# Attention scores in 32x32 tiles, |Kh| steps on ScalarE, reordered engines and filler matmuls in a one-core transformer layer

## The reference

```python
g, v = x @ Wg.T + bg, x @ Wv.T + bv            # 16 heads of 8 features
corr = (g_i . g_j) / (|g_i| |g_j| + 1e-8) * m  # m: j <= i and j >= i - 128
corr = (corr + 1) / 2
gene_means = mean over j of corr;  denom = gene_means + 0.5
fitness = 1 / (denom * sum_i(1 / denom))
attn = softmax over j of (corr * fitness_i * m + (1 - m) * -1e10)
x1 = layernorm(x + (attn @ v) @ Wo.T + bo)
gate, up = fp4(x1) @ fp4(Wgate).T, fp4(x1) @ fp4(Wup).T   # 352 wide
h = silu(gate) * up
out = layernorm(x1 + fp4(h) @ fp4(Wdown).T)
```

## Time and profile before

| | |
|---|---|
| median of 3 runs | 390.52 us (386.58 to 390.61) |
| the profiled execution | 388.84 us, its span 387.0 us |
| PE busy | 329.3 us (85%), 2964 matmuls |
| DVE busy | 285.6 us (74%) |
| ACT busy | 223.8 us (58%) |
| POOL busy | 188.2 us (49%) |

### The profile page before, as it was taken

The page is one execution under the profiler, slowest core; times in us unless marked ns, Lnnn a source line. Parts: engine busy times, 40 slices in busy tenths (PEclk is TensorE's granted clock), DMA queues, the critical chain, the costliest instruction groups (busy, mean ns, idle before and its releaser), DMA issues.

```text
span 387.0 us, 8906 instructions
## 1 busy us (share of the span) xinstructions
PE 329.3 (85%) x2964; PEld 196.2 (51%) x2964; DVE 285.6 (74%) x820; ACT 223.8 (58%) x499; POOL 188.2 (49%) x466
## 2 busy tenths in 40 slices
PE   6368878798899999999999999999998999967542
PEld 4234444454455565655565555555554556635331
DVE  1535356667879797979797979797979798886751
ACT  2034564566667776767676767777776777513210
POOL 7754033507274747374737373737373333541441
PEclk9999998899999999999999999999999999985655
DMA  4001000000010101010101010100000000000000
GB/s 117 27 1 29 14 2 3 27 2 29 0 30 3 42 1 42 0 46 1 42 0 45 1 43 2 43 0 30 3 30 0 29 3 27 15 0 14 15 14 19
DMA packets 12405, 7.64 MB, mean 20 GB/s; under 512 B 1026, under 2 KB 12356, under 8 KB 12356
## 3 DMA queue, kind: packets, MB, share of 16 engines
q1 hardware_dynamic: 12356, 7.03, 6.4%
HBM read 4.93 MB, written 2.10 MB: 18 GB/s over the span
## 4 chain that ended last, share of the span: by engine, by line
PE 30%; DVE 23%; POOL 20%; issue 17%; ACT 8%; POOLq 0%; ACTq 0%; DVEq 0%
PE OT L745 6%; PE S L722 5%; PE WA L871 4%; POOL nt L463 4%; PE S L726 3%; ACT Pm L561 3%; POOL rstd L496 3%; POOL nt L465 3%; POOL rn L470 3%; POOL nt L468 2%; DVE A L1274 2%; POOL B L510 2%; DVE xn L1166 2%; PE WB L784 2%; DVE h L1118 2%
## 5 line engine op out<-in xcount | busy, mean ns | idle before, releaser
L561 ACT ACTIVATE Pm<-S 128x384 f32<-128x384 f32 x256 | 111.7, 490 | 64.0 <-PE S L726 63.9
L722 PE MATMUL S<-mask,ident 128*128 128x384 f16 x256 | 65.8, 340 | 10.0 <-ACT Pm L561 7.8
L745 PE MATMUL OT<-Pm,gv 128*32 128x256 f32 (+1 forms) x1024 | 56.8, 341 | 0.0
L487 POOL TENSOR_TENSOR hq<-hm,hs 128x352 f32<-128x352 f32 x32 | 25.2, 789 | 63.8 <-DVE hm L1136 63.6
L726 PE MATMUL S<-BT,AT 32*128 32x256 f16 (+1 forms) x512 | 44.3, 252 | 0.0
L745 PEld LDWEIGHTS OT<-Pm,gv 128*32 128x32 f32 x1024 | 27.2, 111 | 21.4 <-issue 6.0
L726 PEld LDWEIGHTS S<-BT,AT 32*128 32x128 f16 x512 | 14.4, 93 | 43.0 <-issue 43.0
L722 PEld LDWEIGHTS S<-mask,ident 128*128 128x128 f16 x256 | 18.9, 99 | 33.7 <-issue 14.8
L840 PE MATMUL WD<-wdT,hqT 128*128 128x128 f32 (+1 forms) x192 | 29.5, 311 | 1.5 <-ACT hqT L614 1.5
L840 PEld LDWEIGHTS WD<-wdT,hqT 128*128 128x128 f32 (+1 forms) x192 | 26.3, 217 | 4.1 <-ACT hqT L614 2.2
L1112 DVE SCALAR_TENSOR_TENSOR hh<-th,WC 128x352 f32<-128x352 f32 x29 | 15.0, 518 | 17.7 <-ACT th L585 17.6
(11 more groups left out here) (160 smaller groups left out, 724.4 us busy)
## 6 DMA issues: line engine op xcount, KB each, us to landing
xT<-x_turned_dram SPq DMA_DIRECT2D x16, 128.0 KB, 2.2
x_res<-x_dram SPq DMA_DIRECT2D x16, 128.0 KB, 2.1
out_dram<-yo SPq DMA_DIRECT2D x16, 128.0 KB, 2.1
wf<-w_down_dram SPq DMA_DIRECT2D x1, 176.0 KB, 2.6
wgv<-wgv_dram SPq DMA_DIRECT2D x1, 128.0 KB
wf<-w_gate_dram SPq DMA_DIRECT2D x1, 128.0 KB, 2.2
wf<-w_up_dram SPq DMA_DIRECT2D x1, 128.0 KB, 2.2
woT<-wo_dram SPq DMA_DIRECT2D x1, 64.0 KB
```

The lines of the kernel that those rows point to most:

```text
L487: pool.tensor_tensor(b3(hq[:, k, 0:I]), b3(hm[:, k]), bc(hs[:, k], QB), ALU.mult).then_inc(s_hq, 1)
L561: act.activation(Pm[:, group % PR, hd % 4, :], S[:, (H * x + hd) % 3, 0:SCW], ACT.Exp, scale=1.0 / ZS).then_inc(s_exp, 1)
L722: pe.matmul(S[:, bank, 0:SCW], ident16[:, :], mask16[:, :], start=True, stop=False)
L745: i = pe.matmul(OT[VP * g:VP * (g + 1), T - (q1 - q0):T], gv_flat[:, at:at + VP], Pm[:, (GROUPS * x + c) % PR, g, q0:q1], start=(kt == 0 a ...
```

## The change

Scores: instead of the mask over everything and two wide matmuls per head, each head takes twelve matmuls with 32 contraction rows and 32 output rows: for each 32 keys only the queries that the window lets them meet (160 columns for the first 128 keys, 128, 96, 64 and 32 for the second), and then a mask of three 32-column blocks for each 32 keys on top. What lies outside is never written: DVE sets it to -60000 once at the start. Rounding of h: ACT computes |2^22 * hn - 4| (hn has its sign turned over by a negative factor), and DVE needs two combined operations (max with the constant, then add or subtract) where it had four. Orders: POOL does all three Newton steps together, then the high half of B, then `rstd`, and both halves of `h_over_scale` later; ACT takes gsq and gv before values_out 0 and exponentials 6; DVE takes gh before the scale of h, the low half of A behind all of quant_x, and the three steps of gene_size in between those of the fitness, ahead of gate and up. `keep_busy` puts three 128x384 matmuls whose results are overwritten before the hq transposes, before the attention transpose, and before gate/up k=0.

```diff
+            def keep_busy(bank):
+                for _ in range(3):
+                    pe.matmul(bank[:, 0:SCW], ident16[:, :], mask16[:, :], start=True, stop=True)
...
             pair = [(2 * p + k, (H * x + 2 * p + k) % 3) for k in range(2)]
-            for hd, bank in pair:
-                pe.matmul(S[:, bank, 0:SCW], ident16[:, :], mask16[:, :], start=True, stop=False)
-            for kt, (q0, q1) in enumerate(((0, T), (T, SCW))):
+            for kt in range(NT):
                 for hd, bank in pair:
                     r, c = 32 * (hd % 4), hd // 4
-                    i = pe.matmul(S[:, bank, q0:q1], AT[r:r + 32, x % 2, c, kt * P:(kt + 1) * P],
-                                  BT[r:r + 32, x % 2, c, T - (q1 - q0):T], start=False, stop=(kt == 1))
-                    if kt == 1:
-                        i.then_inc(s_sc, 1)
+                    for k0 in range(0, P, KG):
+                        at, n = (k0, P + KG) if kt == 0 else (T + k0, P - k0)
+                        q = kt * P + k0
+                        pe.matmul(S[k0:k0 + KG, bank, at:at + n], AT[r:r + 32, x % 2, c, q:q + KG],
+                                  BT[r:r + 32, x % 2, c, q:q + n], start=(kt == 0), stop=False)
+            near = mask16[:, :].rearrange("p (b c) -> p b c", c=P)
+            for n, (hd, bank) in enumerate(pair):
+                m = 32 * (hd % 4)
+                for k0 in range(0, P, KG):
+                    i = pe.matmul(S[k0:k0 + KG, bank, 0:SCW].rearrange("p (b c) -> p b c", c=P)[:, :, k0:k0 + KG],
+                                  ident16[m:m + KG, m:m + KG], near[m:m + KG, :, m:m + KG],
+                                  start=False, stop=True)
+                i.then_inc(s_sc, 1)
...  PE's order
             scores(t, 2)
             after_last(pe, (t - 3, s_h, h_done(t - 3)))
+            keep_busy(WC)
             ... transposes of hq
             after_last(pe, *wc_last)
+            keep_busy(WC)
             pe.wait_ge(s_attn, t)
             ... transpose of attention
+            after_last(pe, (t - 4, s_ln2, 5 * (t - 4) + 1), (t - 3, s_h, h_done(t - 3)))
+            keep_busy(WD)
             pe.wait_ge(s_xac, copied(t) + (t == B))
-            after_last(pe, (t - 4, s_ln2, 5 * (t - 4) + 1), (t - 3, s_h, h_done(t - 3)))
...  POOL's order
-            newton(t + 2, (0, 1, 2) if t < 0 else (0,))
-            rstd(t - 2, ...)
+            newton(t + 2)
             B16 high half of t + 1
-            newton(t + 2, (1, 2))
-            h_over_scale(t - 3, 0)
+            rstd(t - 2, ...)
             A16 high half of t + 2
+            h_over_scale(t - 3, 0)
             h_over_scale(t - 3, 1)
             h_times_scale(t - 3, 0)
...  ACT
+            def step_of_h(x, k):
+                act.wait_ge(s_hn, NT * x + k + 1)
+                act.activation(hu[:, k], hn[:, k], ACT.Abs, bias=off[:, :], scale=STEP).then_inc(s_hu, 1)
             exps(t, 4)
+            step_of_h(t - 3, 0)
             BT copy of t + 1
+            step_of_h(t - 3, 1)
             exps(t, 5)
             xaT copy
-            values_out(t, 0)
-            exps(t, 6)
             gsq, gv of t + 3
+            values_out(t, 0)
+            exps(t, 6)
             tanh(t - 2, 0)
...  DVE: the old order and the new one, what moves
-  gate/up(t-3,1), h_scale 0, B low half, h_scale 1, gh, h_scale 2
+  gate/up(t-3,1), gh, h_scale 0, B low half, h_scale 1, h_scale 2
-  quant_x 0 to 5, A low half, quant_x 6 to 8, round_h(0) 4 steps
+  quant_x 0 to 8, A low half, round_h(0) 2 steps
-  gw, rs, den, rden; gate(t-2,0), gene_size 0, up(t-2,0), gene_size 1, 2
+  gene_size 0, gw, gene_size 1, rs, gene_size 2, den, rden; gate(t-2,0), up(t-2,0)
```

More of the change, by code:

```diff
@@ L32 @@
 MASKED = -60000.0
+KG = 32
 ZS = 256.0
@@ L35 @@
 UNNUDGE = 1.0 - 2.0 ** -22
+STEP, STEP_OFF = 2.0 ** 22, -4.0
 LN_EPS = 1e-5
@@ L236, in layer @@
         s_hrn = sem("s_hrn")
+        s_hu = sem("s_hu")
+        s_off = sem("s_off")
         s_hn = sem("s_hn")
@@ L450, in bias_rows, with newton @@
                 pool.wait_ge(c_pool, 30)
-            def newton(x, steps):
+            def newton(x):
                 y0 = rn[:, :]
@@ L456, in newton @@
                 sd = seed[:, :].bitcast(F32)
-                for k in steps:
+                for k in range(3):
                     src = sd if k == 0 else y0
@@ L510, in _ @@
                     pool.tensor_copy(B16[:, :, 0:3:2, :], twice(Bf)).then_inc(s_Bhi, 1)
-                if live(t + 2) and t >= 0:
-                    newton(t + 2, (1, 2))
-                if live(t - 3):
-                    h_over_scale(t - 3, 0)
+                if live(t - 2) and t != B + 1:
+                    rstd(t - 2, mv1, ve1, rstd1, nm1, nb1, s_ln1, 5 * (t - 2) + 5, s_rs1)
                 if live(t + 2):
@@ L574, in values_out @@
                 act.activation(OTs[:, half, :], OT[:, 0:T], ACT.Copy).then_inc(s_ot, 1)
+            def step_of_h(x, k):
+                if x == 0 and k == 0:
+                    act.wait_ge(s_off, 1)
+                act.wait_ge(s_hn, NT * x + k + 1)
+                act.activation(hu[:, k], hn[:, k], ACT.Abs, bias=off[:, :], scale=STEP).then_inc(s_hu, 1)
             def apply_1(t):
@@ L1006, in _ @@
         def _(dve):
+            for k0 in range(0, P, KG):
+                for a, b in ((0, k0), (k0 + P + KG, T), (T, T + k0)):
+                    if a < b:
+                        dve.memset(S[k0:k0 + KG, :, a:b], MASKED).then_inc(s_far, 1)
             dve.wait_ge(ld_b, 16 * 3)
@@ L1106, in residual_2, with low_B @@
                                   WD[:, 0:T].rearrange("p (n d) -> p n d", n=NT), ALU.add).then_inc(s_ln2, 1)
+            def low_B(x):
+                dve.wait_ge(s_Bhi, x + 1)
+                need(dve, s_B, x)
+                dve.tensor_tensor(B16[:, :, 1:4:2, :], twice(Bf), B16[:, :, 0:3:2, :], ALU.subtract).then_inc(s_Blo, 1)
             def gate(x, k):
@@ L1219, in _ @@
                     ln_aggr(t - 4, s_ln2, st2, mv2)
+                if t < 0 and live(t + 1):
+                    low_B(t + 1)
                 if live(t - 3):
@@ L1244, in _ @@
                 if live(t - 3):
+                    h_scale(t - 3, 0)
+                if t >= 0 and live(t + 1):
+                    low_B(t + 1)
+                if live(t - 3):
+                    h_scale(t - 3, 1)
                     h_scale(t - 3, 2)
-                if t == B:
+                if live(t - 2) and t < B:
+                    for step in range(4):
+                        quant_x(t - 2, step)
+                if live(t - 1):
                     dve.wait_ge(s_ob, t)
@@ L1249, in _ @@
                     dve.reciprocal(orec[:, :], o[:, :, HD]).then_inc(s_on, 1)
+                if live(t - 2) and t < B:
+                    quant_x(t - 2, 4)
+                if live(t - 1):
                     dve.wait_ge(s_on, t)
@@ L1252, in _ @@
                     dve.tensor_tensor(attn[:, :, :], o[:, :, 0:HD], bc(orec[:, :], HD), ALU.mult).then_inc(s_attn, 1)
[L1253 to L1269, removed]
-                    quant_x(t - 2, 5)
-                if live(t + 2):
-                    dve.wait_ge(s_Ahi, t + 3)
-                    need(dve, s_A, t + 2)
-                    dve.tensor_tensor(A16[:, :, 2:4, :], twice(gh), A16[:, :, 0:2, :], ALU.subtract).then_inc(s_Alo, 1)
-                if live(t - 2) and t != B + 1:
+                if t == B:
+                    for step in range(5):
+                        quant_x(t - 2, step)
+                if live(t - 2) and t <= B:
+                    quant_x(t - 2, 5)
                     quant_x(t - 2, 6)
@@ L1280, in _ @@
                     down_weights()
+                if live(t + 2):
+                    dve.wait_ge(s_Ahi, t + 3)
+                    need(dve, s_A, t + 2)
+                    dve.tensor_tensor(A16[:, :, 2:4, :], twice(gh), A16[:, :, 0:2, :], ALU.subtract).then_inc(s_Alo, 1)
                 if live(t - 3):
                     round_h(t - 3, 0, 0)
[L1284 to L1285 removed]
                 if live(t - 4) and t != B + 1:
@@ L1294, in _ @@
                     ln_sums(B - 1, s_ln1, y, st1)
+                    ln_aggr(B - 1, s_ln1, st1, mv1)
                 if live(t - 3):
                     round_h(t - 3, 1, 0)
-                if t == B:
-                    ln_aggr(B - 1, s_ln1, st1, mv1)
                 if live(t - 4) and t != B + 1:
                     ln_aggr(t - 4, s_ln2, st2, mv2)
+                if live(t - 3):
+                    round_h(t - 3, 1, 1)
+                early_genes = live(t + 3) and t >= 0
+                if early_genes:
+                    gene_size(t + 3, 0)
                 if live(t + 2):
@@ L1307, in _ @@
                                       WB[:, 0:T], ALU.mult).then_inc(s_fit, 1)
-                if live(t - 3):
-                    round_h(t - 3, 1, 1)
+                if early_genes:
+                    gene_size(t + 3, 1)
                 if live(t + 2):
@@ L1312, in _ @@
```

(13 more changed lines are left out.)

51 lines of the change are left out of this document (19 added, 32 removed).

## The result

The changed kernel takes 367.0 us (median of 4, 362.74 to 368.89) against 390.27 before: ratio 0.9397, 95% interval 0.9313 to 0.9482. The forecast was 361 us in a range of 345 to 386. The profiled execution took 368.89 us with a span of 367.0, 20.0 less than the span of before. The ratios leave out executions more than 1.5% above the fastest of their kernel (here the profiled one, 368.89 against 362.74), which the medians keep.

What follows compares the result with a forecast made beforehand. PE's work (18.7 us) and a loop over all engines nearly tied; PE's 18.7 - 2.56 + 1.5 = 17.65 us saves 1.7 a period, 26.5 over 15.5 periods, plus 1.5 in the tail: 361 us, range 345 to 386.

Steps and rivals of the forecast that it cites:

- Scores: On PE, a pair of scores falls from 0.70 to 0.38 us; eight pairs gain 2.56 us a period.
- 7 ns launches of four tiles: In `values`, four weight loads with their matmuls cover 0.13 us, starting about 7 ns apart; 24 launches would take 0.17 us.
- Rival 2: On PE, launches of the score tiles bind: at 25 ns a pair takes 0.79 us, total 412 us; chance 0.14.
- Fillers: On PE, nine matmuls of 384 columns, 0.17 us each, cost 1.5 us a period; bounds 0.7 and 1.5.
- rival 3: Fillers cost nothing because PE waits at their places; the period falls to 16.9 us, total 349 us; chance 0.12.
- The loop: Over all engines from xm through seed, Newton, B, rstd, apply and quant_x: 16.8 us, against 19.4 in the old kernel.
- rival 1: The loop or ACT's coupling to PE binds instead: period 18.4 us, 15.5 us gained, total 373 us; chance 0.18.
- Rounding: Rounding of h: DVE does 1.4 us less, 15.0 us a period; ACT gets 0.95 more, 14.9 us.
- Orders: On POOL, rstd and B move behind Newton: gh comes 2.0 us earlier, rstd 3 us later after the seed.
- under PE's slack: The low half of B comes later on DVE without cost, since turn B is a pair and more behind.
- The first and last not full: Scores of 16 sequences make 16 periods, the first and last partial: 15.5 x 1.7 = 26.5 us gained.
- a clock under 1.00: Sign of being wrong: granted clock below 1.00 between 100 and 330 us, meaning tiled matmuls count for less.

Runs made afterwards that it cites:

- the split Newton: The changed kernel with POOL's old order: Newton step 0, then rstd of the first norm and high half of B, then steps 1 and 2; 420.97 us, ratio 1.0854.

## Why the prediction held, point by point

**Direction, range and period were right; the limiter was wrong.** The sum set PE's 17.65 us above a loop of 16.8. Measured, PE's work is 16.6 and the loop 17.42. The forecast period was off by only 0.23 us because two errors cancelled, which is luck.

- **Scores.** 8 x 0.32 = 2.56 us was forecast, 2.9 measured. The estimate of 0.19 us for entry and exit came from a pair with two tile shapes in it. A pair with one shape pays about 0.11 within its 0.28 us, and five of eight pay another 0.1 in the group ahead: 0.34 us a pair on average, where the sum had 0.38. The 7 ns launches of four tiles carried over, and better: 3 ns. Rival 2 is out. The rule of the Trainium skill (TensorE: Matmul & The Clock Gate, "Wait — 56ns, not 53.3ns?") of 25 ns between starts does not hold between different tiles, which start 3 ns apart here. What the same page of the Trainium skill has on packed tiles ("Measured speedup vs the span model"), about 4 ns for each further tile, agrees with the 3 ns.
- **Fillers.** 1.5 us forecast on the path; they add 1.0 to PE's work and nothing to the time, as removing them shows. Their place in the sum was wrong, since PE is not the limit: that they cost nothing came true of rival 3, though PE waits ahead of the sum and not at their places.
- **The loop.** 16.8 us forecast, 17.42 measured; this is rival 1's mechanism with a smaller price. Two loops lie side by side, and the forecast's sum had only the one over POOL. Its terms are read from POOL and DVE of the changed kernel:

```profile
159.50 0.78 POOL L494 TENSOR_TENSOR hq<-hm,hs 128x352 f32<-128x352 f32 x1
160.25 0.23 POOL L470 TENSOR_TENSOR nt<-seed 128x32 f32<-128x32 f32 x1
...
166.62 0.39 POOL L505 TENSOR_TENSOR nb<-nm,rstd 128x2 f32<-128x2 f32 x1
```

```profile
159.32 0.17 DVE L1102 TENSOR_SCALAR seed<-seed 128x32 int32<-128x32 int32 x1
...
167.95 0.42 DVE L1196 TENSOR_REDUCE xmax<-y 128x16 f32<-128x256 f32 x1 [0.44 <-ACT y L571]
...
171.66 0.43 DVE L1215 TENSOR_TENSOR xm<-xn,xs 128x256 f32<-128x256 f32 x1
```

  From xm (ends 154.66) to the seed (159.49) 4.8 us, as forecast. Then POOL is still at hq, and Newton starts 0.76 later: the term that the sum did not have, since hq now ends next to the seed. Newton to nb 160.25 to 167.01, 6.8 (6.85 forecast), apply and hand-over 0.9, quant_x 4.1. The missing 0.76 us, less some small change, is the 0.6 us by which this loop was undersized. The other loop runs from DVE's 1/denominator over PE's sum, output projection, values, scores, gate/up and turn A to ACT, y1 and quant_x; the profile's chain for this period takes this way and not the one over POOL, and the forecast had no term for it. The two meet at y1, where `nb` is ready at 167.01 and ACT comes to it at 167.04. Taking 0.49 us out of the loop over PE brought 0.23; the loop over POOL then binds alone at 17.2, still with hq ahead of Newton.
- **Rounding.** 1.4 us of DVE's work was booked as work under a limit elsewhere. It lies on the loop in full, and undoing it costs 3.4 us a period, 1.9 on DVE and 1.5 by the clock's fall.
- **Orders.** Forecast as 2 us off the path between seed and gh; with wide scores the period falls by 0.8 until PE binds. That gh now heads DVE's order and with it the low half of B was noted only as "under PE's slack"; the split Newton shows that it is not.
- **The head** was the step that failed. "The first and last not full" let it gain part of 1.7 us a period; it lost 5.2. The forecast did not ask what PE's shorter work does to its clock there. Rows of before hinted at it: a pair starts after waits of 0.6 to 1.0 us in the head, and until 42 us and around 65 and 72 us its matmuls run at 1.2 GHz. That fillers there bring 8 us shows the clock to be the cause. The prediction named a clock under 1.00 as a sign of being wrong, but only between 100 and 330 us.

Sum of the errors in the profiled execution: periods 19.2 gained over ten, a little over the forecast's 17; end 6.1; head -5.2. Forecast 28, measured 20.0. The changed kernel's four runs spread over 6 us; the heads of its relatives without extra work there (projection of t = 2 between 80.0 and 87.3 us) spread as much, so the head is the likely cause, which was not measured on the same kernel.

## What to carry to other kernels

Where PE's work and a loop over the other engines are about as long, shortening one of them can cost time: with the tiles alone PE idled 2.5 us in one lump, came out at half clock, and the work behind the wait, which lies on the loop, took nearly twice as long (1.91 us and not 1.03). Shorten the loop first, then PE, and put work whose result is thrown away into the lumps that stay, above all in the head, where the waits are. In an in-order queue, add up for each hop also what the receiving engine has queued ahead of it at that moment (here hq before Newton), and look for every way round the loop, not only the one that the change shortens.

## What the runs showed of the hardware

- Matmuls in 32x32 tiles at eight places of the array start 3 ns apart with their weight loads. 24 of them, 384 columns, take 0.28 us from start to start with the way out; two heads in wide form took 0.70. The way in lengthens the full-array group ahead by 0.09 to 0.13 us.
- With tiles alone, where each period had a wait of PE of 2.5 us, half clock followed each of them between 100 and 290 us. A wait of that length was not followed by it every time: behind the 2.61 us of the split Newton shown above PE ran on at full clock, and the wait of 3.28 us for the weights, at 71 us, was followed by half clock in the changed kernel (three fp32 transposes in 0.85 us) and by full clock with twice the fillers (0.52). In the kernels whose waits were 0.4 to 0.9 us a period the clock stayed at 1.00 from 120 to 280 us.
- With the same instructions on PE up to 60 us, the clock had risen at 44 us in one execution (no fillers) and not yet at 60 us in another (the changed kernel).
- Three filler matmuls, 0.50 us from their start to what follows, lengthened PE's queue by 0.40, 0.18 and 0.44 us at the three places. At gate/up the difference is that the fp32 matmuls behind them start 0.1 us sooner than right behind row tiles.
